# Three adjacency buffers in the mask pass, and the halves of the normalised rows made under it

## The reference

```
n = adj with its diagonal removed                 # node_adj_norm and edge_adj_norm
node_support = n @ h                              # h is the layer norm of x
for each of 3 heads:
    hW = h @ W;  hp = (n > 0) @ hW;  hm = (n < 0) @ hW
    e_plus = leaky_relu([hp, hm] @ a);  e_minus = leaky_relu([hm, hp] @ a)
    att = softmax over each row of (e_plus where n > 0, e_minus where n < 0, else -9e15)
    edge_support += (att * n) @ hW
out = de * GRU_e(node_support, h) + dn * GRU_n(edge_support / 3, h)
```

## Time and profile before

| | |
|---|---|
| three runs | 2088.46, 2084.15, 2087.63 us (median 2087.63) |
| profiled execution | 2086.31 us, span 2084.7 us |
| busy, PE / DVE / ACT / POOL | 1813.1 / 1646.8 / 1336.4 / 221.6 us |
| chain that ended last | PE 51%, DVE 3%, ACT 2%, POOL 1% of the span |
| mask pass and layer norm | 0 to about 200 us |
| from there to the first attention tile | about 200 to 329 us |
| loads of adj into Ar | 32 of 2,048 KB, median 13.2 us to landing |

### The profile page before, as it was taken

The page is one execution under the profiler, slowest core; times in us unless marked ns, Lnnn a source line. Parts: engine busy times, 40 slices in busy tenths (PEclk is TensorE's granted clock), DMA queues, the critical chain, the costliest instruction groups (busy, mean ns, idle before and its releaser), DMA issues.

```text
span 2084.7 us, 27839 instructions
## 1 busy us (share of the span) xinstructions
PE 1813.1 (87%) x8959; PEld 875.8 (42%) x9108; DVE 1646.8 (79%) x1393; ACT 1336.4 (64%) x1428; POOL 221.6 (11%) x163
## 2 busy tenths in 40 slices
PE   2511697999999999999998899999998989997997
PEld 2511242444444444444446344444454334455443
DVE  7544777988988998989567687878768988856998
ACT  4766136887887887888334656555546877735775
POOL 2000201000101011001441000000006910000000
PEclk6555798999999999999996999999998999988999
DMA  8998037445445446444500311111002069922321
GB/s 334 390 422 302 37 108 260 152 151 169 154 154 175 150 149 183 139 152 151 207 0 0 94 51 40 50 40 50 1 21 121 0 282 429 422 76 92 104 102 68
DMA packets 75387, 311.83 MB, mean 150 GB/s; under 512 B 12969, under 2 KB 21641, under 8 KB 65567
## 3 DMA queue, kind: packets, MB, share of 16 engines
q1 hardware_dynamic: 75314, 310.88, 41.7%
HBM read 297.88 MB, written 12.98 MB: 149 GB/s over the span
## 4 chain that ended last, share of the span: by engine, by line
PE 51%; DVE 3%; ACT 2%; issue 2%; POOL 1%; ACTq 0%; DVEq 0%; POOLq 0%
PE psum L1114 13%; PE psum L1126 13%; PE psum L1199 8%; PE psum L1062 8%; PE psum L1087 1%; PE psum L1089 1%; PE psum L891 1%; PE psum L1177 1%; DVE prod L1722 1%; PE psum L1101 1%; PE psum L886 1%; POOL halves L577 1%; PE psum L897 1%; PE psum L1091 1%; PE psum L1092 1%
## 5 line engine op out<-in xcount | busy, mean ns | idle before, releaser
L717 ACT ACTIVATE ss<-KR,cls 128x1024 bf16<-128x1024 int16 x384 | 413.0, 1138 | 106.6 <-DVE pl L1557 106.5
L1062 PE MATMUL psum<-ph,Tt 128*128 128x512 bf16 x1503 | 411.2, 380 | 8.5 <-DVE pl L1557 6.8
L795 ACT ACTIVATE hid<-psum,fB 128x1024 f32<-128x1024 f32 x208 | 227.1, 1112 | 184.2 <-PE psum L1114 184.1
L1114 PE MATMUL psum<-hTp,fW 128*128 (+1 forms) x1202 | 285.0, 383 | 11.9 <-ACT hid L795 4.0
L1126 PE MATMUL psum<-hidp,fW 128*128 128x512 bf16 x1241 | 279.5, 379 | 2.3 <-DVEq L1688 1.9
L1554 DVE TENSOR_TENSOR ph<-ss,Ahi 128x3072 bf16<-128x3072 bf16 x128 | 228.5, 1785 | 55.3 <-PE psum L1062 55.2
L1666 DVE TENSOR_TENSOR hidp<-hid,hidp 128x1024 bf16<-128x1024 f32 x208 | 245.4, 1221 | 26.6 <-ACT hidp L789 26.0
L1062 PEld LDWEIGHTS psum<-ph,Tt 128*128 128x128 bf16 x1536 | 149.8, 98 | 190.8 <-DVE pl L1557 7.1
L1557 DVE TENSOR_TENSOR pl<-ss,Alo 128x3072 bf16<-128x3072 bf16 x128 | 227.2, 1775 | 0.0
L1062 PE MATMUL psum<-pl,Tt 128*128 128x512 bf16 x753 | 226.0, 380 | 0.8
L1114 PEld LDWEIGHTS psum<-hTp,fW 128*128 128x128 bf16 x1248 | 117.0, 98 | 169.1 <-ACT hid L795 31.9
(11 more groups left out here) (231 smaller groups left out, 2121.9 us busy)
## 6 DMA issues: line engine op xcount, KB each, us to landing
Ar<-in_adjT SPq DMA_DIRECT2D x32, 2048.0 KB, 13.2
Ab<-in_adjT SPq DMA_DIRECT2D x128, 512.0 KB, 4.0
A<-in_adjT SPq DMA_DIRECT2D x32, 2048.0 KB, 10.5
Tt<-T_d SPq DMA_DIRECT2D x128, 256.0 KB, 2.6
mB<-mk_d SPq DMA_DIRECT2D x64, 512.0 KB, 3.7
T_d<-tb SPq DMA_DIRECT2D x32, 192.0 KB, 1.9
RD<-rden_d SPq DMA_DIRECT2D x12, 512.0 KB, 5.8
fWs<-in_W SPq DMA_DIRECT2D x2, 2304.0 KB, 15.6
```

The lines of the kernel that those rows point to most:

```text
L717: last = nc.scalar.activation(ss[s % 2][:, h, :], KR[:, h, rb * RB:(rb + 1) * RB], ACT.Sigmoid, scale=STEP, bias=cls[:, ds(t * HEADS + h, 1)])
L795: nc.scalar.activation(hid[j % HB][:, :], flat[:, j % 2 * CW:j % 2 * CW + CW], func, bias=fB1[:, j:j + 1]).then_inc(act_done[k], 1)
L1062: last = nc.tensor.matmul(psum[:, 2 * h + q, :], Tt[s % AS][:, h, w, :], mv[:, q * CH:(q + 1) * CH], start=fresh and k == 0, stop=False, s ...
L1114: last = nc.tensor.matmul(psum[:, j % 2 * 2 + b, :], fW[0][x][:, j * P:(j + 1) * P], hTp[y][:, ds(q * CW + b * CH, CH)], start=(w == 0), s ...
```

## The change

The mask pass gets three `Ar` buffers. The 16 KB of the fourth (from 176 KB) hold `hTs` from now on, which can then be written while the pass runs and `hT` is still in place. `acc6` moves to 160 KB and `lw` to 192 KB. ACT copies a quarter of `hT` to `hTs[0]` after each of tiles 8 to 11, POOL subtracts each quarter right then, and fills `acc6` when ACT has finished tile 29. DVE waits for the four subtracts before tile 20, the first whose mask lies over `hT`. The reload into `hT2` is gone, and the counts on `th_in` and `range_g` follow.

```diff
-MS = 4
+MS = 3
...
-        lw = sb("lw", [P, NT, P], BF16, 176)
+        lw = sb("lw", [P, NT, P], BF16, 192)
...
-        acc6 = sb("acc6", [6, N], F32, 184)
+        acc6 = sb("acc6", [6, N], F32, 160)
...
-        hT2 = sb("hT2", [P, N], F32, 128)
...
-        hTs = [sb(f"hTs{i}", [P, N], BF16, 160 + 8 * i) for i in range(2)]
+        hTs = [sb(f"hTs{i}", [P, N], BF16, 176 + 8 * i) for i in range(2)]
...
-        m_in = S("m_in0", "m_in1", "m_in2", "m_in3")
+        m_in = S("m_in0", "m_in1", "m_in2")
...
             sp.wait_ge(m_neg, NT)
-            sp.dma_start(hT2[:, :], hT_d).then_inc(th_in, 16)
             sp.dma_start(gw[:, :], a["gatW"]).then_inc(th_in, 16)
...
+            for i in range(4):
+                c = slice(i * RB, (i + 1) * RB)
+                pool.wait_ge(th_hi, i + 1)
+                pool.tensor_tensor(hTs[1][:, c], hT[:, c], hTs[0][:, c], ALU.subtract).then_inc(th_lo, 1)
+            pool.wait_ge(m_neg, NT - 2)
+            pool.memset(acc6[:, :], 0.0).then_inc(range_g, 1)
+
             pool.wait_ge(range_l, 1)
...
-            pool.wait_ge(th_in, 32)
+            pool.wait_ge(th_in, 16)
             pool.tensor_copy(gwb[0][:, :], gw[:, :]).then_inc(pool_hi, 1)
             pool.wait_ge(pool_hi, 3)
             pool.tensor_tensor(gwb[1][:, :], gw[:, :], gwb[0][:, :], ALU.subtract).then_inc(th_lo, 1)
-            pool.wait_ge(lv_w, 1)
-            pool.wait_ge(th_hi, 1)
-            for i in range(4):
-                c = slice(i * RB, (i + 1) * RB)
-                pool.tensor_tensor(hTs[1][:, c], hT2[:, c], hTs[0][:, c], ALU.subtract).then_inc(th_lo, 1)
-            pool.memset(acc6[:, :], 0.0).then_inc(range_g, 1)
...
             for n in range(5, NT):
                 negative(n)
+                if 8 <= n < 12:
+                    act.wait_ge(ln_done, 2)
+                    c = slice((n - 8) * RB, (n - 7) * RB)
+                    nc.scalar.activation(hTs[0][:, c], hT[:, c], ACT.Copy).then_inc(th_hi, 1)
...
-            act.wait_ge(th_in, 32)
-            nc.scalar.activation(hTs[0][:, :], hT2[:, :], ACT.Copy).then_inc(th_hi, 1)
...
                 if n == NT // 2 + 4:
                     dve.wait_ge(spilled, 32)
+                    dve.wait_ge(th_lo, 4)
                 mask(n)
...
-            dve.wait_ge(range_g, 1)
+            dve.wait_ge(range_g, 2)
...
-            dve.wait_ge(range_g, 2)
+            dve.wait_ge(range_g, 3)
...
-                dve.wait_ge(range_g, 3)
                 gather(0)
```

More of the change, by code:

```diff
@@ L1028, in _ @@
             with pe.If(nsign == 2):
-                pe.wait_ge(th_in, 48)
+                pe.wait_ge(th_in, 32)
                 for t in range(NT):
```

## The result

The changed kernel takes 2090.79 us (median of 12 runs, 2084.86 to 2097.66), the kernel before 2086.64 on the same chip (12 runs, 2084.15 to 2090.05). The ratio is 1.0022 with a 95% interval from 1.0013 to 1.0031: slower by 2.7 to 6.5 us, where 2.0 less were forecast. The time itself, 2090.79, lies just inside the stated range of 2080.0 to 2091.0. The profiled execution took 2092.54 us with a span of 2090.7, 6.0 more than the span before.

The account below looks back on a forecast made before the run. It took DMA to bound the mask pass and a DVE-PE chain the level sums behind it. Terms -9.1 - 0.2 + 0.5 + 4.9 + 1.1 + 0.5 + 0.3 = -2.0 us gave 2085.6 us, range 2080.0 to 2091.0.

Parts of the forecast that it names:

- Three buffers, in steady state: Mask pass from tile 13 on: three buffers need 4.80 us per tile, DMA needs 4.89, so it just fits; 0.5 us lost.
- A beat over 5.0: Sign of a wrong prediction: mask-pass tiles more than 5.0 us apart, where 4.9 was expected from tile 12 on.
- The three-buffer round is too long: Rival, SP's issue behind ACT in the mask pass: landing 9.5 us, 5.30 per tile, +5.3 us, 2092.9; chance 0.12.
- The start: Start of the mask pass: one tile fewer loaded early costs 4.9 us, a later issue after tile 5 another 1.1.
- The level sums: First level sums behind the pass: without POOL's subtracts beside DVE, PE never waits; gain 9.1 us.
- Work under the pass: ACT's copies, POOL's subtracts and the zero fill in the mask pass fall into DVE's waits; 0.3 us lost.
- POOL takes the pass: Rival, mask pass: each POOL instruction holds DVE for its length; +7.7 us, 2095.3; chance 0.05.
- The end of the pass: Last mask tile: it lands late already, the change keeps the load order, so its 2.5 us delay stays.
- The first rival: Mask pass: only the one tile is lost and the last tile's 2.5 us delay goes; -6.9 us, 2080.7; chance 0.25.

Follow-up runs that it names:

- ACT's cut: ACT's sum of negatives cut to 128 of 4096 columns from tile 12 on: in the changed kernel 2081.75 us, in the kernel before (four buffers) 2082.67 us.

## Why the prediction was wrong

**The step that failed** is "Three buffers, in steady state". It took the landing of a lone tile, 8.0 us, for the landing of a tile in a stream, found (6.4 + 8.0) / 3 = 4.80 under the DMA's 4.89, and put 0.5 us down. In the stream of the changed kernel a landing takes 9.3 to 10.2 us, the round becomes 5.35 a tile, and the term was 9.5 us instead of 0.5. The row that spoke for it, the 10.2 us of the tile issued at 50.6, was set aside as queueing beside the spill of T_d. In the changed kernel the spill goes out only at 62.18, and the tile issued at 50.9 lands at 61.6, after 10.7 us all the same. A beat over 5.0 was among the prediction's own signs of being wrong. The rival "The three-buffer round is too long" had the mechanism, the landing (9.5) and nearly the beat (5.30), its price of 7.8 us and +5.3 in all; the spans differ by 6.0. It was given 0.12.

**The start** (4.9 + 1.1) was right: tile 11 is 6.0 us later (7.2 with three buffers alone, of which 0.7 are there at tile 0). **The level sums** were right in kind and size: 9.0 measured alone. In the changed kernel 7.3 of it are left, for three reasons that together come to a little more than the missing 1.7. The fill holds the last mask for 0.5 us (2.77, not 2.29). POOL's subtract on gw holds a level weight for 0.6 (1.27, not 0.68); I had priced this pair at 0.5, but on the instructions ahead of the weights. And the first group takes 9.8 us, 0.9 more than before; the time that PE needs there after its idle time varied between 8.4 and 9.8 in these profiles.

**Work under the pass** (0.3) was right to within the 1.4 us that the kernel with three buffers alone leaves open, but only in part for the reason given. Two of the four subtracts did meet a mask and not a wait of DVE, and DVE, which had begun first, kept its 2.29 us while POOL's instruction grew from 2.1 to 2.40 and 3.22:

```profile
100.19 2.29 DVE L1227 TENSOR_SCALAR keep<-Ar 128x4096 fp8e4<-128x4096 f32 x1
101.24 3.22 POOL L507 TENSOR_TENSOR hTs<-hT,hTs 128x1024 bf16<-128x1024 f32 x1 [2.78 <-ACT hTs L636]
```

The rival "POOL takes the pass" falls with it. **The end of the pass** was wrong by 2.2 us in the good direction: the last tile comes 5.1 us after the one before. The first rival had this part, and its reason, the length of the queue between the two loads, fits: with queues standing ahead it was late again (by 1.3 and 0.8 us with ACT's cut). No run took the diagonal's load away, so the reason stays unproven.

**The sum by its own terms:** -9.0, +1.7 given back in the stretch, +6.0, +9.5, -2.2 make +6.0. The range reached up to 2091.0 because of the doubt about the landing, and the time lies 0.2 below that end. That is partly luck: without the 2.2 us at the last tile, which the sum did not have, the same error would have led past it. The direction was wrong.

The two places on the Trainium skill: the stream's landing is 9.6 us, the lone tile's 8.0, and the estimate from the Trainium skill's DMA: Bandwidth & Descriptors (Anatomy of one DMA), 6.8 us, was the farthest off. At the fill DVE's mask began while POOL was at work and took 2.77 us, and at the subtract above DVE began first and POOL's instruction grew. Both agree with the rule of the Trainium skill's SBUF — State Buffer (Who interferes with whom), that of a POOL instruction and a DVE instruction in a two-port mode the one that issues first has the shared ports and the other blocks; which mode the masks ran in the traces do not say.

## What to carry to other kernels

A ring of buffers keeps a DMA stream full only if (holding time + landing) / buffers stays under the time of one transfer, and the landing to put in is that of a tile with as many others in flight as the ring will have: here 9.6 us with three buffers, not the 8.0 of a lone one. Where the spare comes out at a few per cent, treat the buffer as needed. Before giving a buffer away to move POOL's work out of DVE's way, try to let DVE do it where PE is still busy: DVE did the four subtracts in 4.7 us under PE's matmuls, kept the fourth buffer, and beat both kernels.

## What the runs showed that was not expected

A DMA share near 1.00 is not a full pipe. Over 50 to 80 us of the pass the kernel before moves 428 GB/s at a share of 1.01 (120 to 180 us), the changed kernel 379 at 0.97 (150 to 200 us), and two buffers 289 at 0.79 (160 to 240 us). Per busy time that is about 424, 391 and 366 GB/s: the fewer loads in flight, the longer the same bytes keep the engines busy. Why the packets of a shallow queue take longer, the runs leave open.

POOL's subtract of 384 columns starts 6.9 to 7.3 us after its cast has ended, in every one of these profiles. A gap in DVE's chain of weights is not what released it: in the changed kernel it starts at 232.19, in the middle of that chain (the first group's last weight ends at 234.13), in the kernel before 0.3 us after the chain's end. POOL's streams in the section on the change have an instruction (ISA) between the cast and the subtract; whether the time is its own, no run shows.
